# Attention and a quantised feed-forward on one core: the first unit's statistics, butterflies and turns in earlier batches, three roundings on ScalarE, the next input's turn ahead of a wait

## The reference, cut to what matters

```
x = x + tanh(g_xattn) * attention(layernorm(x), ctx, ctx)          # 16 batches, 128 tokens, 512 wide, 32 q heads, 8 kv heads of 16
x = x + tanh(g_ffn)   * ffn(layernorm(x))

h_bitlinear(x, w) = act_quant(fwht(x)) @ weight_quant(w).T
  fwht         normalised Walsh-Hadamard transform along the last axis
  act_quant    scale = 127 / max(|x|) per token; round(x * scale) clipped / scale
  weight_quant scale = mean(|w|); round(w / scale) clipped to -1, 0, 1, * scale
ffn(h) = h_bitlinear(silu(h_bitlinear(h, w_gate)) * h_bitlinear(h, w_up), w_down)     # 512 -> 2048 -> 512
```

## Time and profile before

| | |
|---|---|
| median of 3 runs | 470.04 us |
| profiled execution | 473.62 us, its span 471.8 us |
| granted TensorE clock | 0.992 of full speed |
| busy TensorE / VectorE / ScalarE / GpSimd | 96% / 82% / 62% / 46% |
| attention | to about 175 us |
| gate and up rows of units 1 to 4 | from 175.2, 238.0, 312.4, 386.5 us |
| end of the last products | 468.5 us |

### The profile page before, as it was taken

The page is one execution under the profiler, slowest core; times in us unless marked ns, Lnnn a source line. Parts: engine busy times, 40 slices in busy tenths (PEclk is TensorE's granted clock), DMA queues, the critical chain, the costliest instruction groups (busy, mean ns, idle before and its releaser), DMA issues.

```text
span 471.8 us, 9054 instructions
## 1 busy us (share of the span) xinstructions
PE 455.3 (96%) x3108; PEld 292.4 (62%) x3128; DVE 386.3 (82%) x715; ACT 293.1 (62%) x522; POOL 216.6 (46%) x335
## 2 busy tenths in 40 slices
PE   9999999999999989989999999999999999999997
PEld 8755555555555534468944479864468874479664
DVE  5778998787877749868998967999885999889891
ACT  3378897677777788777647417643616663647460
POOL 4235646889898454655005734202926300930000
PEclk9799999999999999999999999999999999999999
DMA  8999020121013241000200651100361110153086
GB/s 240 328 348 350 18 57 13 24 58 24 13 24 102 23 123 78 2 0 14 24 11 1 111 135 33 22 12 0 67 156 46 24 24 0 29 92 60 1 139 218
DMA packets 68183, 35.90 MB, mean 76 GB/s; under 512 B 50288, under 2 KB 62960, under 8 KB 68144
## 3 DMA queue, kind: packets, MB, share of 16 engines
q1 hardware_dynamic: 67408, 34.48, 29.0%
q10 hardware_dynamic: 736, 0.92, 0.7%
HBM read 19.26 MB, written 4.19 MB: 50 GB/s over the span
## 4 chain that ended last, share of the span: by engine, by line
PE 70%; DVE 10%; POOL 7%; issue 6%; ACT 4%; DMA 2%; ACTq 0%; DVEq 0%; POOLq 0%
PE ps L879 16%; PE ps L956 11%; PE ps L933 9%; PE ps L608 7%; PE ps L630 4%; PE ps L673 4%; PE ps L690 3%; PE ps L945 2%; PE ps L947 2%; PE ps L822 2%; PE ps L638 2%; DMA x_all<-in_x 2%; DVE y_split L1453 2%; DVE mz L1492 1%; PE ps L732 1%
## 5 line engine op out<-in xcount | busy, mean ns | idle before, releaser
L879 PE MATMUL ps<-wst 128*128 128x512 bf16 x499 | 111.7, 380 | 3.2 <-DVE wst L1473 2.0
L1310 DVE TENSOR_REDUCE reg<-ps 128x4 f32<-128x512 f32 x128 | 81.7, 683 | 25.6 <-PE ps L630 24.0
L879 PEld LDWEIGHTS ps<-wst 128*128 128x128 bf16 x512 | 49.1, 98 | 62.1 <-DVE wst L1473 3.9
L572 POOL TENSOR_TENSOR reg_rest<-reg_rest,z_sc 128x1024 f32<-128x1024 f32 x24 | 47.3, 2008 | 84.6 <-DVE z_sc L1515 84.6
L1037 ACT ACTIVATE reg<-ps 128x512 f32<-128x512 f32 x116 | 62.9, 596 | 26.5 <-PE ps L638 25.4
L630 PE MATMUL ps<-reg 32*128 32x256 f32 x512 | 74.2, 405 | 0.7 <-DVE reg L1310 0.7
L1173 ACT ACTIVATE wst<-wst 128x512 f32<-128x512 f32 x64 | 40.0, 626 | 51.3 <-DVE wst L1473 51.0
L608 PE MATMUL ps<-reg 32*128 32x512 f32 x232 | 70.1, 639 | 0.0
L933 PE MATMUL ps<-had_f,wst 128*128 128x128 f32 x512 | 67.1, 276 | 1.1 <-DVE wst L1478 1.1
L933 PEld LDWEIGHTS ps<-had_f,wst 128*128 128x128 f32 x512 | 64.0, 192 | 4.3 <-DVE wst L1478 1.8
L1203 ACT CAST y_split<-ps 128x512 fp32r<-128x512 f32 x64 | 37.3, 584 | 36.3 <-PE ps L933 36.3
(11 more groups left out here) (173 smaller groups left out, 766.1 us busy)
## 6 DMA issues: line engine op xcount, KB each, us to landing
wst<-in_w SPq DMA_DIRECT2D x16, 512.0 KB, 8.0
reg<-in_w SPq DMA_DIRECT2D x8, 512.0 KB, 5.7
out<-x_all SPq DMA_DIRECT2D x16, 256.0 KB, 2.1
x_all<-in_x SPq DMA_DIRECT2D x3, 1024.0 KB, 9.2
reg<-in_v SPq DMA_DIRECT2D x4, 256.0 KB, 3.6
reg<-in_k_t SPq DMA_DIRECT2D x28, 32.0 KB, 2.7
x_all<-in_x ACTq DMA_DIRECT2D x1, 512.0 KB, 7.6
reg_rest<-reg SPq DMA_TRANSPOSE x20, 3.0
```

The costliest lines, as they stand in the source:

```text
L572: pool.tensor_tensor(z, z, sc, ALU.mult).then_inc(sem("z_scaled"), 1)
L879: last = pe.matmul(ps[:, banks[ob % n], :], tern_gu[:, ob // 2, m, j, P * (ob % 2):P * (ob % 2) + P], q1_t[:, j, :], start=(j == 0), stop= ...
L1310: dve.tensor_reduce(neg_max[n % 2][:, g:g + 2, i + m, :], ps[:, row_bank(r, m), :].rearrange("p (g a t) -> p g a t", g=2, a=2), AX_X, ALU. ...
```

## The change

Tables: the front of the first unit's batches 0 to 3 goes from attention steps 5, 7, 9, 11 to 4, 5, 6, 7; the turns, Hadamard products and spreads one step earlier each. `last_steps` loses the Hadamard product of step 14 and has the spread in step 14 in place of 15. ScalarE rounds the small Hadamard matrix (`round_had16`) after step 5 in place of 6.

Gate and up stage: ScalarE takes three of the eight roundings, after places 8, 10 and 12 (two after 9 and 11 before); VectorE makes one behind its last gate (place 15) and four after the loop. The chain starts ahead of the up rows of place 4, VectorE's part is at place 4 (5 before), the way back stands ahead of the gate rows of place 7, and VectorE's end of it ahead of gate 7.

Transform: the turn of the next unit's first batch stands ahead of the wait for the last hidden product, in place of after the first four products.

```diff
-        EARLY_TURN = {7: 0, 9: 1, 11: 2, 13: 3}
-        EARLY_HAD = {8: 0, 10: 1, 12: 2, 14: 3}
-        EARLY_SECOND = {9: 0, 11: 1, 13: 2, 15: 3}
+        EARLY_TURN = {6: 0, 8: 1, 10: 2, 12: 3}
+        EARLY_HAD = {7: 0, 9: 1, 11: 2, 13: 3}
+        EARLY_SECOND = {8: 0, 10: 1, 12: 2, 14: 3}
...
-        FRONTS = {5: 0, 7: 1, 9: 2, 11: 3}
+        FRONTS = {4: 0, 5: 1, 6: 2, 7: 3}
...
-        ROUND_ACT = {9: 0, 11: 1}
+        ROUND_ACT = {8: 0, 10: 1, 12: 2}
+        ROUNDED_ACT, ROUNDED_DVE = 3, 5
...
 def last_steps():                       # TensorE
                 weigh(b - 1, 1)
-                early_had(b)
                 quarter(b, 1)
...
                 weigh(b, 0)
+                early_second(b)
                 turn_out(b - 1, 1)
                 b = NB - 1
...
                 weigh(b, 0)
-                early_second(b)
                 turn_out(b - 1, 1)
...
 def quantise_input(u, step):            # TensorE
-                    if step == FIRST_TURN[tb]:
+                    if tb > 0 and step == FIRST_TURN[tb]:
...
 def gate_up(u, chain, first):           # TensorE
+                    if chain is not None and ob == 7:
+                        chain_back(chain)
                     if ob < NC - 1:
                         rows(u, chain, ob, 0, "g_done", G_BANKS, "gs_done")
-                    if chain is not None and ob == 7:
-                        chain_back(chain)
+                    if chain is not None and ob == 4:
+                        chain_start(chain)
...
                     rows(u, chain, ob, 1, "u_done", U_BANKS, "h_done")
-                    if chain is not None and ob == 4:
-                        reach_apart(pe, sem("ones_set"), (sem("mz_done"), ...), (sem("y_low"), ...))
-                        pe.transpose(ps[0:NG, 4, 0:P], mz[:, :], ident_f[:, :]).then_inc(sem("c_t1"), 1)
...
 def transform(u, nxt):                  # TensorE
+                if nxt is not None:
+                    reach(pe, sem("gs_done"), u.times(NC, NC - 1))
+                    first_turn(batch(nxt, 0), 0)
                 reach(pe, sem("h_done"), u.times(NC, NC))
...
-                if b == 6:              # ScalarE, attention
+                if b == 5:
                     round_had16()
...
 def gates_and_chain(u, prev):           # VectorE
+                    if prev is not None and ob == 7:
+                        chain_end(prev)
                     gate(u, ob)
+                    if prev is not None and ob == NC - 1:
+                        rounding(prev, ROUNDED_ACT)
...
-                    if prev is not None and ob == 7:
-                        chain_end(prev)
...
-                        if ob == 5:
+                        if ob == 4:
                             chain(prev)
-                        if 12 <= ob < 14:
-                            rounding(prev, ob - 10)
-                        if more and ob >= 14:
-                            rounding(prev, ob - 10)
...
-                rounding(Index(i, 0), 6)
-                rounding(Index(i, 0), 7)
+                for p in range(4, 8):
+                    rounding(Index(i, 0), p)
```

More of the change, by code:

```diff
@@ L345, in turn @@
             def turn(u, p, q2, q=q_z):
-                if u < NU - 1 and p < 2:
-                    sp.wait_ge(sem("rounded_act"), 2 * u + p + 1)
+                if u < NU - 1 and p < ROUNDED_ACT:
+                    sp.wait_ge(sem("rounded_act"), ROUNDED_ACT * u + p + 1)
                 elif u < NU - 1:
-                    sp.wait_ge(sem("rounded"), 6 * u + p - 1)
+                    sp.wait_ge(sem("rounded"), ROUNDED_DVE * u + p + 1 - ROUNDED_ACT)
                 else:
-                    sp.wait_ge(sem("rounded"), 6 * u + p + 1)
+                    sp.wait_ge(sem("rounded"), ROUNDED_DVE * u + p + 1)
                 sp.dma_start_transpose(q2[:, 8 * p:8 * p + 8, :], q[:, 8 * p:8 * p + 8, :].rearrange("p g a -> p (g a)")
@@ L909, in gate_up, with chain_start @@
                     rows(u, chain, ob, 1, "u_done", U_BANKS, "h_done")
-                    if chain is not None and ob == 4:
-                        reach_apart(pe, sem("ones_set"),
-                                    (sem("mz_done"), chain.times(8, 8)),
-                                    (sem("y_low"), chain.times(16, 16)))
-                        pe.transpose(ps[0:NG, 4, 0:P], mz[:, :], ident_f[:, :]).then_inc(sem("c_t1"), 1)
+            def chain_start(u):
+                reach_apart(pe, sem("ones_set"),
+                            (sem("mz_done"), u.times(8, 8)),
+                            (sem("y_low"), u.times(16, 16)))
+                pe.transpose(ps[0:NG, 4, 0:P], mz[:, :], ident_f[:, :]).then_inc(sem("c_t1"), 1)
             def chain_back(u):
@@ L1191, in rounding @@
                 act.activation(z, z, ACT.Identity, bias=p_magic[:, :]).then_inc(sem("lifted"), 1)
-                reach(act, sem("lifted"), u.times(2, p + 1))
+                reach(act, sem("lifted"), u.times(ROUNDED_ACT, p + 1))
                 act.activation(q_z[:, 8 * p:8 * p + 8, :], z, ACT.Identity, bias=m_magic[:, :]).then_inc(sem("rounded_act"), 1)
@@ L1207, in evacuate @@
                         if nxt is None:
[L1208 to L1209 removed]
+                            if z // 2 < ROUNDED_ACT:
+                                act.wait_ge(sem("rounded_act"), ROUNDED_ACT * (NU - 2) + z // 2 + 1)
                             else:
[L1211 removed]
+                                act.wait_ge(sem("rounded"), ROUNDED_DVE * (NU - 2) + z // 2 + 1 - ROUNDED_ACT)
                         act.copy(Z[:, 4 * z:4 * z + 4, :].rearrange("p g a -> p (g a)"),
@@ L1546, in _, with gates_and_chain @@
                 step(b)
-            def gates_and_chain(u, prev, more=False):
+            def gates_and_chain(u, prev):
                 reach(dve, sem("a2_done"), u.times(16))
                 for ob in range(NC):
+                    if prev is not None and ob == 7:
+                        chain_end(prev)
                     gate(u, ob)
+                    if prev is not None and ob == NC - 1:
+                        rounding(prev, ROUNDED_ACT)
                     if ob == 1 and prev is None:
                         dve.wait_ge(sem("signed"), 12)
-                    if prev is not None and ob == 7:
-                        chain_end(prev)
                     if ob > 0:
@@ L1585, in _ @@
                 split_and_inputs(Index(i, 0), Index(i, 1))
-                gates_and_chain(Index(i, 1), Index(i, 0), more=True)
-                rounding(Index(i, 0), 6)
-                rounding(Index(i, 0), 7)
+                gates_and_chain(Index(i, 1), Index(i, 0))
+                for p in range(4, 8):
+                    rounding(Index(i, 0), p)
                 for tb in range(UB):
```

## The result

The changed kernel takes **472.44 us** (median of 10 runs, 471.47 to 477.41) against 470.04 (median of 10 runs of the kernel before beside them); the ratio is 1.0056, with a 95% interval of 1.0034 to 1.0078. It is slower by 2.4 us by the medians, 2.6 by the ratio, where 0.75 less was forecast, and it lies outside the range of 466.5 to 472.0. Two things make this up, and the granted TensorE clock of each execution separates them: the five at 0.999 or 1.0 take 471.47 to 471.89, 1.6 us more than before; the other five show 0.989 to 0.996 and take 1.3 to 5.7 us more still.

A forecast was written before the change was run, and what follows sets the result against it. TensorE was taken to bound the kernel, so only its few idle microseconds could be won. Attention +0.8, gate/up -1.5, projections +0.2, turn -0.45 and +0.2 sum to -0.75 us on the 470.04 median: 469.3 us, range 466.5 to 472.0.

The forecast's parts named there:

- What bounds the kernel: TensorE; only its idle can be won: waits of 2.4 (butterflies), 2.0 (gate products), 1.2 (ScalarE copy), 1.1 us (hidden product).
- Middle of attention, +1.7: Attention: GpSimd's work drawn together in steps 4 to 7 makes TensorE wait in steps 8 and 9; +1.7 us.
- the weight sum's wait is swallowed: Attention, values of batch 6: a wait of up to 0.8 us, swallowed by the later 2.4 us scales wait.
- The single waits: Attention: first turn waits 0.85 us for butterflies, step 8's spread 2.4 for scales, step 9's selectors 0.65 for split maxima.
- End of attention, -0.9: Last attention steps: idle of 1.20 us before the transposes goes, ScalarE's copy and late maxima add 0.3; net -0.9 us.
- Roundings and chain, -1.5 + 0.2: Gate/up stage gains 0.5 us in each of three units; two projections lose 0.1 each to later roundings.
- Rival C: Projections: the rounding behind the last gate takes 2.24 us and lands 1.0 late in two; 471.2 us, chance 0.17.
- the sum was to be 1.0 higher: Gate/up stage: if VectorE and GpSimd lock each other out, the loop's one remaining rounding lands 0.5 us later; sum 1.0 higher.
- The turn ahead of the wait, -0.45 + 0.2: Transform: the next input's turn gains 0.45 us in the first unit, costs 0.1 in each of the next two.
- The turn fits in: First unit: TensorE idles 1.1 us before the transform, butterflies are long done, so the turn fits there; -0.45 us.
- A: Attention: GpSimd's lateness stays off the path; attention -2.3, in all -3.85, 466.2 us; chance 0.2.
- B: Attention: GpSimd's lateness lasts, each 3% more adds 1.1 us on step 8's spread, selectors of 10, 11 wait; 471.3, chance 0.23.

The follow-up runs named there:

- experiment 7: Kernel before with the attention changes alone, VectorE's statistic of step 6 moved behind the weight sum; 474.09 us, ratio 1.0081.
- experiment 2: Also called the control: changed kernel with attention's tables as before, keeping roundings, chain and the turn ahead of the wait; 469.34 us, ratio 0.9995.
- experiment 1: Kernel before with the attention changes alone (fronts in steps 4 to 7, tables one step earlier, new last steps); 472.04 us, ratio 1.0047.
- experiment 3: Kernel before with only the changed roundings and chain places, attention and the next input's turn as before; 468.59 us, ratio 0.9969.
- experiment 8: Experiments 5 to 7 together plus the change's roundings and chain, measured against the kernel before; 482.98 us, ratio 1.027.
- experiment 10: Experiment 2 with the turn of the next input's second batch one place later in the transform; 469.08 us, ratio 0.9998.
- experiment 6: Experiment 1 with GpSimd's two scales moved ahead of the butterflies of the same step; 473.5 us, ratio 1.0116.
- experiment 5: Experiment 1 with the four fronts two steps apart, in steps 4, 6, 8, 10; 477.61 us, ratio 1.014.
- experiment 12: Experiment 11 plus experiment 7's moved statistic and experiment 3's roundings and chain, no turn ahead of the wait; 469.48 us, ratio 0.9986.
- experiment 9: Experiment 5 with GpSimd's shifted weight halves redistributed: one in steps 7, 9, 11, 13, two in 8, 10, 12, 14; 470.93 us, ratio 1.0019.
- experiment 11: Experiment 1 with one front moved from step 7 to 8 (fronts in 4, 5, 6, 8); 471.35 us, ratio 1.0056.

## Why the prediction was wrong

- **What bounds the kernel**: right. The four waits of the earlier trace rows are those that moved.
- **Middle of attention, +1.7**: the step that failed, in size and not in mechanism. GpSimd's queue sets the spread of step 8, as forecast, and the weight sum's wait is swallowed by that (experiment 7, on one execution). Measured +2.8, and the 1.1 missing are in two places. GpSimd's steps 5 to 7 took 36.0 us (10.70, 11.24 and 14.03) where the sum had 35.4: it was added up from single rows, without the small gaps between them, and two halves took 2.34 us, not 2.2. So on the clock of the trace of before the spread starts at 109.1, not 108.5, and the selectors at 113.1, not 112.4; after what the butterflies' waits give back, as forecast, 0.5 is left of that. The other 0.6 is VectorE's, at the end of step 11 and in step 13, where a product of 0.21 us took 0.90 and 0.82 beside GpSimd's halves. The sum had nothing for step 11; what it had for step 13, 0.3, stands in its next term.
- **The single waits**: first turn 0.66 where 0.85 was forecast, selectors 0.33 against 0.65, scales 1.54 against 2.4. That 1.54 and the 0.85 for the weight sum make 2.39 is in part luck: TensorE reached the spread 1.5 us later than forecast (0.5 at the start of step 8 and 1.0 within it, where the first batch's rounding, which the sum had left at nothing, makes the maxima late), and GpSimd's scales came 0.6 later.
- **End of attention, -0.9**: -0.67 from the products of batch 14 to the first gate row (8.52 us against the control's 9.19), as 0.55 of the idle 1.20 stays (L691), and with the 0.3 of step 13 it is -0.4. The first unit's rows are 0.24 shorter, which the sum didn't have and which isn't explained. Attention in all: 2.83 - 0.67 - 0.24 = +1.9, which is experiment 1, where the sum had +0.8.
- **Roundings and chain, -1.5 + 0.2**: right, -1.28 by experiment 3. The gate/up stage is 0.4 to 0.5 us shorter in each of three units (29.27 to 29.28 us against 29.68 to 29.76 in experiment 1), each projection 0.06 longer. The rounding behind the last gate took 0.85 us, not 1.2. Rival C is refuted. The Trainium skill, "SBUF — State Buffer", section "Who interferes with whom", has VectorE in a two-port mode and GpSimd lock each other out for a whole instruction; by that rule the sum was to be 1.0 higher. The roundings don't test this: in experiment 3 the one behind the last gate starts at 262.76, and GpSimd's last multiplication ends at 263.06. In attention the trace agrees: the product of 128x2 values that ends with GpSimd's half (138.27 and 138.24) is held as by such a lock; whether it runs in that mode the trace doesn't say.
- **The turn ahead of the wait, -0.45 + 0.2**: wrong, +0.75 (experiment 2 less experiment 3) and +2.9 by itself. "The turn fits in" the first unit's gap, but the transform isn't shorter for it. In the others the step counted only the wait (0.85 us without the earlier statistics, as it said: 0.8) and not that the turn, moved ahead of the transform, delays its start by 0.5 us of its own without making it shorter.
- **Clock**: not in the forecast at all. It adds about 0.8 us to the median.
- **Rivals**: A is refuted. B had the mechanism of the miss: "each 3% more" of GpSimd's work on the spread (it was 2%, and its step 7 ended at 109.0), and the right sign. But it had other waits behind it: no selector of steps 10 and 11 waited. Its 471.3 is 0.4 below the executions at full clock.

The sum at full clock: 1.9 for attention by itself, -1.3, +0.75, in all +1.4, where +1.6 is measured; 0.2 us is not assigned. The Trainium skill, "Perfetto Trace Analysis", section "Identifying the Most-Contended Engine", sends one to the engine of highest occupancy; GpSimd, busy 46% of the span, set the largest wait of attention all the same (1.54 us).

## What to carry to other kernels

When work is drawn together in time, add it up on every engine that takes part, and lay it over what each engine has by parity or table in those steps; take a term from the start of one step to the start of the next, so that gaps are in it. An engine whose results free buffers shows its lateness as later starts and not as a wait. Then ask of each loss whether a later wait swallows it: here 0.85 us (by experiment 7) and 1.0 us (by the rows) ahead of the spread cost nothing, because GpSimd's queue set its time. An instruction moved ahead of a wait costs its whole length in a stretch without a gap, and what it leaves behind need not get shorter for it (30.8 us with the turn or without). Compare two profiles from a point behind which they differ, and test with a control that has one part undone: the raw spans here had the wrong sign.

## What was not expected of the hardware

A standstill of TensorE in mid-kernel can be followed by a stretch at its lower clock, 0.50 of full speed, for about 3 us. The traces show two kinds of such stretches. One lies before 28 us, in work that all kernels share (the traces of before, at 0.992, and of experiments 7, 8 and 10; with nothing else it gives 0.988 in experiment 10). The other lies behind a long wait in attention: one such fall gives 0.996 (the traces of experiments 1 and 6), two give 0.993 (experiment 5).

| longest wait in attention, us | kernels | executions below 0.999 |
|---|---|---|
| 1.14 | experiment 12 | 0 of 11 |
| 1.20 | before, in 71 executions with a listed clock | 7, all at 0.985 to 0.989 |
| 1.28 | experiment 9 | 0 of 12 |
| 1.54 | the changed kernel and experiment 1 | 7 of 15, five of them at 0.996 |
| 1.82 | experiment 6 | 6 of 6 |
| 2.8, in the profiled execution | experiment 7 | 12 of 13 |
| 2.54, with one of 2.14 | experiment 5 | 6 of 6 |
| 4.1, in the profiled execution | experiment 8 | 7 of 7 |

One fall in attention costs 1.2 to 1.4 us, by the medians (472.96 against 471.78 in experiment 1; 473.1 against 471.68 in the changed kernel). Experiments 5 and 9 differ in the waits through one table, and the falls come and go with them; that is the strongest evidence that the standstill is the cause. The longest wait alone doesn't tell it, though: in experiment 11 no wait in attention is over 0.85 us in the profiled execution, and 5 of 12 still lose clock, and experiment 2, with the attention of before, has one execution of 12 at 0.993. What is lost there stays open.
